# The last norm of an experts stage moved from VectorE to ScalarE, a tile per unit, its statistics spread over three units

## The chip, the cores and the metric

One core of a Trainium2 chip runs the whole program. The metric is device microseconds of one execution, as the median of several runs. The engines are named in the profile as PE (TensorE matmul), PEld (its weight loads), DVE (VectorE), ACT (ScalarE), POOL (GpSimd) and SP (SyncE, which here issues all DMAs). Each engine works through its own queue in order, and waits on semaphores that other engines raise.

## The reference

The program is a decoder of six sub-layers over 8192 tokens of width 128, each followed by a residual add and a layer norm without gain. The change touches the last, a mixture of experts with a shared expert:

```python
x = _layernorm(x + _L1_ffn_ref(x, ...), axis=-1)      # the output

def _layernorm(x, axis=-1, eps=1e-05):
    m = jnp.mean(x, axis=axis, keepdims=True)
    v = jnp.var(x, axis=axis, keepdims=True)
    return (x - m) / jnp.sqrt(v + eps)

# _L1_ffn_ref: 64 experts of inner width 64, a router's weight coef per token and expert
g = jnp.einsum('th,ehi->tei', x, Wg)
u = jnp.einsum('th,ehi->tei', x, Wu)
h = jax.nn.silu(g) * u * coef[:, :, None]
moe_out = jnp.einsum('tei,eih->th', h, Wd)
shared = jax.nn.silu(x @ SWg) * (x @ SWu) @ SWd       # inner width 128
return (moe_out + shared).reshape(orig_shape)
```

## The kernel before

The experts are computed in `phase_moe`, the last stage of the program. Tokens are taken 512 at a time (a group; 16 groups, `steps` = 8 turns of `U` = 2). The 64 experts go in 32 pairs of 2 x 64 inner columns, and the shared expert is the 33rd, so a group has `UNITS` = 33 units. Within a unit, everything is transposed: features or inner columns on the 128 partitions, 512 tokens along the free axis. Values are split into a high and a low f16 part, and each product is three f16 matmuls (`thrice`).

The steps of unit u, by engine:

- PE, `up`: 6 matmuls from `x_high` and `x_low` into two PSUM tiles `ps_g` and `ps_u`, of which there are two each. It therefore waits until the unit two before has been read out of them, by ScalarE (`silu_ready`) and by VectorE (`upper_ready`).
- ACT, `gate`: silu of `ps_g` into `gated`.
- DVE, `weigh`: `ps_u` times the router's weights (`coef`, loaded by DMA 4 units at a time) into `upper`.
- POOL, `join`: `hidden` = `gated` x `upper`.
- ACT, `high_h`, and DVE, `low_h`: the two f16 parts of `hidden`. Both are issued two units later (`HALVED` = 2).
- PE, `down`: 3 matmuls into the group's PSUM tile `ps_o`, four units later (`LAG` = 4).

So the order in which the queues take their work is, in a unit: PE `up(u)`, `down(u-4)`; ACT `gate(u)`, `high_h(u-2)`; DVE `weigh(u)`, `low_h(u-2)`; POOL `join(u)`. `hidden`, `gated`, `upper` and the f16 parts have `NB` = 6 buffers.

What is left of the previous group is put between the units of the next one, by constants that hold the number of a unit. In unit `COPY_OUT` = 4 ScalarE copies `ps_o` to `oT`. In unit `TURN` = 5 TensorE transposes it back to tokens on partitions, four 128x128 tiles. In unit `ADD` = 6 VectorE adds the residual `x_sb` into `y`, and goes on with four `bn_stats`, four `bn_aggr` and `var_eps` = variance + epsilon. In unit `POWER` = 7 GpSimd raises it to -1/2 (`rstd`). In unit `NORM` = 9 VectorE makes the result, four instructions of one 128x128 tile each:

```python
dve.wait_ge(rstd_ready, nth(it, j))
dve.wait_ge(stored[s], 16 * (it + 1) if j >= 0 else 16 * it)
for q in range(QT):
    last = nc.vector.tensor_scalar(res[s][:, q, :], y[s][:, q, :], mv[s][:, q, 0:1], rstd[s][:, q:q + 1], ALU.subtract, ALU.mult)
```

SyncE stores `res` after it has issued the coefficient loads 0 to 6 of the group's 8 (`store`, on `y_ready`). In unit `PREP` = 16 ScalarE and GpSimd split the next group's `xT` into its parts. After the last group, `drain` does the rest of the work with nothing beside it.

Of the kernel before, what the change touches and what calls it, by code (L numbers as in the profile page):

```python
# [9 lines left out]
ACT = mybir.ActivationFunctionType  # L10
ALU = mybir.AluOpType
# [5 lines left out]
P = 128  # L17
# [2484 lines left out]
def phase_moe(nc, w, x5, x5T, coefT, out):  # L2502
# [6 lines left out]
    U, GROUP, LAG, HALVED = 2, 512, 4, 2  # L2509
    QT = GROUP // P  # L2510
# [1 line left out]
    NB = 6  # L2512
    CU, CBUFS = 4, 4
    CHUNKS = PAIRS_E // CU
    PREP, COPY_OUT, TURN, ADD, POWER, NORM = 16, 4, 5, 6, 7, 9

    with Phase(nc, "d2") as ph:
        def slots(name, shape, dt=F32):
            return [ph.sb(f"{name}{j}", shape, dt) for j in range(U)]
# [9 lines left out]
        oT, y, res = slots("oT", [D, GROUP]), slots("y", [P, QT, D]), slots("res", [P, QT, D])  # L2529
        bn, mv = slots("bn", [P, QT, 6]), slots("mv", [P, QT, 2])  # L2530
        var_eps, rstd = slots("var_eps", [P, QT]), slots("rstd", [P, QT])
        minus_half = ph.sb("minus_half", [P, QT])
        ps_g = [ph.ps(f"g{i}", [P, GROUP]) for i in range(2)]
        ps_u = [ph.ps(f"u{i}", [P, GROUP]) for i in range(2)]
# [3 lines left out]
        coef_loaded = [ph.sem(f"coef_loaded{i}") for i in range(CBUFS)]  # L2538
        stored = [ph.sem(f"stored{j}") for j in range(U)]
        names = ("consts", "x_high_ready", "x_low_ready", "gu_ready", "silu_ready", "upper_ready", "h_ready", "h_high_ready",  # L2540
                 "h_low_ready", "down_done", "oT_copied", "turned", "x_added", "var_ready", "rstd_ready", "y_ready", "dve_own", "waited")
        (consts, x_high_ready, x_low_ready, gu_ready, silu_ready, upper_ready, h_ready, h_high_ready,
         h_low_ready, down_done, oT_copied, turned, x_added, var_ready, rstd_ready, y_ready, dve_own, waited) = (
            ph.sem(n) for n in names)

        def nth(it, j):

            return U * it + j + 1
# [40 lines left out]
        with nc.Block() as block:  # L2589
# [40 lines left out]
            @block.gpsimd  # L2630
            def _(pool):
                nc.gpsimd.memset(minus_half[:], -0.5).then_inc(consts, 1)
                pool.wait_ge(consts, 1)

                def power(it, j):
                    s = j % U
                    pool.wait_ge(var_ready, nth(it, j))
                    nc.gpsimd.tensor_tensor(rstd[s][:], var_eps[s][:], minus_half[:], ALU.pow).then_inc(rstd_ready, 1)

                def low_x(it, j):  # L2640
                    pool.wait_ge(x_high_ready, nth(it, j))
                    if not is_first(it):
                        pool.wait_ge(gu_ready, unit(it, j, UNITS - 1) - UNITS * U)
                    nc.gpsimd.tensor_tensor(x_low[j][:], xT[j][:], x_high[j][:], ALU.subtract).then_inc(x_low_ready, 1)  # L2644

                def join(it, j, u):
                    b = pos(j, u) % NB
                    pool.wait_ge(silu_ready, unit(it, j, u))
                    pool.wait_ge(upper_ready, unit(it, j, u))
                    after(pool, h_low_ready, it, j, u, NB)  # L2650
                    nc.gpsimd.tensor_tensor(hidden[b][:], gated[b][:], upper[b][:], ALU.mult).then_inc(h_ready, 1)  # L2651

                def group(it, j, following, previous):
                    for u in range(UNITS):
                        join(it, j, u)
                        if u == PREP and following is not None:
                            low_x(*following)
                        if u == POWER and previous is not None:
                            power(*previous)
                looped(nc.gpsimd, lambda: low_x(0, 0), group, power)  # L2660
# [48 lines left out]
            @block.scalar  # L2709
            def _(act):  # L2710
                def high_x(it, j):
                    act.wait_ge(xT_loaded[j], 16 * (it + 1))
                    if not is_first(it):
                        act.wait_ge(gu_ready, unit(it, j, UNITS - 1) - UNITS * U)
                    nc.scalar.activation(x_high[j][:], xT[j][:], ACT.Copy).then_inc(x_high_ready, 1)

                def gate(it, j, u):
                    i, b = pos(j, u) % 2, pos(j, u) % NB
                    act.wait_ge(gu_ready, unit(it, j, u))
                    after(act, h_ready, it, j, u, NB)  # L2720
                    nc.scalar.activation(gated[b][:], ps_g[i][:], ACT.Silu, scale=1.0 / W_SCALE).then_inc(silu_ready, 1)  # L2721

                def high_h(it, j, u):
                    b = pos(j, u) % NB
                    act.wait_ge(h_ready, unit(it, j, u))
                    after(act, down_done, it, j, u, NB)
                    nc.scalar.activation(h_high[b][:], hidden[b][:], ACT.Copy).then_inc(h_high_ready, 1)  # L2727

                def copy_out(it, j):
                    s = j % U  # L2730
                    act.wait_ge(down_done, unit(it, j, UNITS - 1))
                    nc.scalar.activation(oT[s][:], ps_o[s][:], ACT.Copy, scale=1.0 / (W_SCALE * H_SCALE)).then_inc(oT_copied, 1)

                def group(it, j, following, previous):
                    for u in range(UNITS):
                        gate(it, j, u)
                        lagging = earlier(it, j, u, HALVED)
                        if lagging is not None:
                            high_h(*lagging)
                        if u == PREP and following is not None:  # L2740
                            high_x(*following)
                        if u == COPY_OUT and previous is not None:
                            copy_out(*previous)

                def drain(it, j):
                    for u in range(UNITS - HALVED, UNITS):
                        high_h(it, j, u)
                    copy_out(it, j)
                looped(nc.scalar, lambda: high_x(0, 0), group, drain)

            @block.vector
            def _(dve):
# [16 lines left out]
                def add(it, j):  # L2769
                    s, number = j % U, nth(it, j)  # L2770
                    dve.wait_ge(turned, number)
                    dve.wait_ge(x_loaded[s], 16 * (it + 1) if j >= 0 else 16 * it)
                    nc.vector.tensor_tensor(y[s][:], ps_o[s][:].rearrange("p (q d) -> p q d", q=QT), x_sb[s][:], ALU.add).then_inc(x_added, 1)
                    dve.wait_ge(x_added, number)
                    for q in range(QT):
                        last = nc.vector.bn_stats(bn[s][:, q, :], y[s][:, q, :])
                    last.then_inc(dve_own, 1)
                    dve.wait_ge(dve_own, 2 * number - 1)
                    dve.sem_inc(waited, 1)
                    for q in range(QT):  # L2780
                        last = nc.vector.bn_aggr(mv[s][:, q, :], bn[s][:, q, :])
                    last.then_inc(dve_own, 1)
                    dve.wait_ge(dve_own, 2 * number)
                    nc.vector.tensor_scalar(var_eps[s][:], mv[s][:, :, 1], EPS_OUT, None, ALU.add).then_inc(var_ready, 1)

                def norm(it, j):
                    s = j % U
                    dve.wait_ge(rstd_ready, nth(it, j))

                    dve.wait_ge(stored[s], 16 * (it + 1) if j >= 0 else 16 * it)  # L2790
                    for q in range(QT):
                        last = nc.vector.tensor_scalar(res[s][:, q, :], y[s][:, q, :], mv[s][:, q, 0:1], rstd[s][:, q:q + 1], ALU.subtract, ALU.mult)  # L2792
                    last.then_inc(y_ready, 1)

                def group(it, j, following, previous):
                    for u in range(UNITS):
                        weigh(it, j, u)
                        lagging = earlier(it, j, u, HALVED)
                        if lagging is not None:
                            low_h(*lagging)  # L2800
                        if u == ADD and previous is not None:
                            add(*previous)
                        if u == NORM and previous is not None:
                            norm(*previous)

                def drain(it, j):
                    for u in range(UNITS - HALVED, UNITS):
                        low_h(it, j, u)
                    add(it, j)
                    norm(it, j)  # L2810
                for j in range(U):
                    dve.sem_inc(stored[j], 16)
                looped(nc.vector, lambda: None, group, drain)
# [105 lines left out]
```

## Time and profile before

| | us |
|---|---|
| median of 3 runs | 4137.38 |
| lowest and highest | 4135.95, 4141.83 |
| the profiled execution, its own time | 4147.94 |
| its span in the trace | 4146.2 |
| TensorE busy in the span | 3539.4 |
| VectorE busy | 3134.3 |
| ScalarE busy | 2357.5 |
| GpSimd busy | 1846.6 |

The experts' stage is roughly the last 1090 us of the span, from 3058.85 us, where its first matmul starts. A line number of the profile is that of `before.py`. In a timeline each row has the start, the duration, the engine, line and operation, out<-in by the program's names (`d_` for this stage's tiles, buffer numbers left out), and in brackets the idle time ahead of it and what ended it. A row with a count above one (x4) merges neighbours: its duration is from the start of the first to the end of the last. Matmuls are pipelined, and their recorded durations overlap.

### The profile page before, as it was taken

The numbers are of one execution on the slowest core, as the hardware profiler recorded it, in microseconds if no ns is written. First come the engines' busy times: TensorE is split into PE (matmuls) and PEld (weight loads), VectorE is DVE, ScalarE is ACT, GpSimd is POOL, SyncE is SP. The second block draws the span as 40 slices with busy tenths as digits, with TensorE's granted clock in tenths as the row PEclk, the third lists the DMA queues.
The fourth block names the chain that finished last, engine by engine and source line by source line (L and its number), as shares of the span: only waits on it lengthen the run. The fifth ranks groups of instructions, "written<-read, shape, count | busy, mean of one in ns | idle before, by whom it ended". The sixth has DMA issues, their size and how long they took to land. (4 is left out here: it accounts for less than half of the span.)

```text
span 4146.2 us, 92196 instructions
## 1 busy us (share of the span) xinstructions
PE 3539.4 (85%) x30917; PEld 2304.7 (56%) x30917; DVE 3134.3 (76%) x6483; ACT 2357.5 (57%) x5257; POOL 1846.6 (45%) x2322
## 2 busy tenths in 40 slices
PE   6899999997675863988999886888759999999998
PEld 3466666664445762666666665777624444444443
DVE  6677777775764654888888885888868888888887
ACT  1455555555672443777777774656545555555555
POOL 1000000002553653556565652222237878787876
PEclk9999999998886875677777777888879999999999
DMA  2000000001112211000000002222165666666664
GB/s 79 7 10 10 10 10 10 10 9 32 46 44 76 66 35 33 16 15 14 15 13 15 15 8 54 57 56 55 46 166 136 139 135 140 133 143 133 136 137 87
DMA packets 279448, 243.73 MB, mean 59 GB/s; under 512 B 57832, under 2 KB 205324, under 8 KB 279308
## 3 DMA queue, kind: packets, MB, share of 16 engines
q1 hardware_dynamic: 267916, 237.21, 24.1%
q10 hardware_dynamic: 11392, 4.79, 0.5%
q8 instruction: 70, 1.15, 0.1%
q14 instruction: 70, 0.57, 0.1%
HBM read 210.34 MB, written 31.59 MB: 58 GB/s over the span
## 5 line engine op out<-in xcount | busy, mean ns | idle before, releaser
L2651 POOL TENSOR_TENSOR d_hidden<-d_gated,d_upper 128x512 f32<-128x512 f32 x528 | 802.7, 1545 | 228.5 <-DVE d_upper L2760 103.5
L2767 DVE TENSOR_TENSOR d_h_low<-d_hidden,d_h_high 128x512 f16<-128x512 f32 x528 | 540.7, 1024 | 119.1 <-ACT d_h_high L2727 117.9
L2721 ACT ACTIVATE d_gated<-d_g 128x512 f32<-128x512 f32 x528 | 315.4, 597 | 461.4 <-PE d_u L2667 461.4
L750 POOL MEMSET f_minus_half<- 128x4 f32 x1 | 0.1, 103 | 866.5 <-POOLq L37 866.5
L2760 DVE TENSOR_TENSOR d_upper<-d_u,d_coef 128x512 f32<-128x512 f32 x512 | 349.3, 682 | 29.0 <-DMA d_coef<-coefT 10.3
L2727 ACT ACTIVATE d_h_high<-d_hidden 128x512 f16<-128x512 f32 x528 | 328.4, 622 | 8.1 <-POOL d_hidden L2651 8.1
L1824 ACT ACTIVATE c_sc<-c_sc,c_negmax 128x129 f32<-128x129 f32 x1024 | 326.2, 393 | 11.7 <-issue 7.7
L1652 POOL TENSOR_TENSOR c_posg<-w_pos,c_gate 128x512 f32<-128x512 f32 x256 | 266.3, 1041 | 0.0
L2665 PE MATMUL d_g<-d_x_high,w_Wg_high 128*128 128x512 f16 x528 | 200.5, 380 | 73.2 <-POOL d_x_low L2644 37.3
L1829 ACT ACTIVATE c_pT<-c_turned 128x512 f32<-128x512 f32 x256 | 149.8, 585 | 156.1 <-PE c_turned L1731 155.9
L1731 PE MATMUL c_turned<-all_ident,c_sc 128*128 128x128 f32 x1024 | 227.2, 361 | 8.2 <-ACT c_sc L1824 7.4
L2665 PE MATMUL d_o<-d_h_high,w_Wd_high 128*128 128x512 f16 x528 | 200.1, 379 | 2.0 <-ACT d_h_high L2727 1.6
L2666 PE MATMUL d_u<-d_x_high,w_Wu_low 128*128 128x512 f16 x528 | 200.4, 379 | 0.0
L2667 PE MATMUL d_u<-d_x_low,w_Wu_high 128*128 128x512 f16 x528 | 200.4, 379 | 0.0
L2665 PE MATMUL d_u<-d_x_high,w_Wu_high 128*128 128x512 f16 x528 | 200.3, 379 | 0.0
L2667 PE MATMUL d_g<-d_x_low,w_Wg_high 128*128 128x512 f16 x528 | 200.3, 379 | 0.0
L2666 PE MATMUL d_g<-d_x_high,w_Wg_low 128*128 128x512 f16 x528 | 200.3, 379 | 0.0
L2667 PE MATMUL d_o<-d_h_low,w_Wd_high 128*128 128x512 f16 x528 | 200.1, 379 | 0.0
L2666 PE MATMUL d_o<-d_h_high,w_Wd_low 128*128 128x512 f16 x528 | 200.1, 379 | 0.0
L1731 PEld LDWEIGHTS c_turned<-all_ident,c_sc 128*128 128x128 f32 x1024 | 147.5, 181 | 65.6 <-issue 49.1
L1936 DVE TENSOR_REDUCE c_top<-c_sc 128x4 f32<-128x516 f32 x256 | 177.0, 691 | 8.8
L1723 PE MATMUL c_scores<-c_rows 24*128 24x128 f16 x1024 | 160.8, 290 | 17.8 <-DVE c_sc L1934 17.7
(409 smaller groups left out, 9900.6 us busy)
## 6 DMA issues: line engine op xcount, KB each, us to landing
d_coef<-coefT SPq DMA_DIRECT2D x256, 512.0 KB, 7.3
d_cT<-in_ctxT SPq DMA_DIRECT2D x128, 64.0 KB, 2.0
mx_x<-in_xT SPq DMA_DIRECT2D x16, 256.0 KB
b_x<-in_x SPq DMA_DIRECT2D x64, 64.0 KB
y<-b_y SPq DMA_DIRECT2D x64, 64.0 KB, 1.6
f_y<-y SPq DMA_DIRECT2D x16, 256.0 KB, 3.3
f_x<-in_x SPq DMA_DIRECT2D x16, 256.0 KB, 3.8
x<-f_res SPq DMA_DIRECT2D x16, 256.0 KB, 2.4
```

The source lines that it names most:

```text
L1652: nc.gpsimd.tensor_tensor(posg[a][:], w["pos"][:, hs, :], gate[s][:, hs].unsqueeze(2).to_broadcast([T, 4, T]), ALU.mult).then_inc(posg_rea ...
L1731: last = nc.tensor.transpose(tbank[a % 2][:, i, :], sc[slot(j)][:, 4 * a + i, 0:T], w["ident"][:])
L1824: last = nc.scalar.activation(sc[s][:, h, :], sc[s][:, h, :], ACT.Exp, bias=negmax[s][:, h:h + 1], scale=SCALE)
L1936: m = own.mark(nc.vector.tensor_reduce(top[s][:, hs], sc[s][:, hs, :], AX, ALU.max))
L2651: nc.gpsimd.tensor_tensor(hidden[b][:], gated[b][:], upper[b][:], ALU.mult).then_inc(h_ready, 1)
L2665: nc.tensor.matmul(out, weights[0], high, start=start, stop=False)
L2666: nc.tensor.matmul(out, weights[1], high, start=False, stop=False)
L2667: return nc.tensor.matmul(out, weights[0], low, start=False, stop=stop)
L2721: nc.scalar.activation(gated[b][:], ps_g[i][:], ACT.Silu, scale=1.0 / W_SCALE).then_inc(silu_ready, 1)
L2727: nc.scalar.activation(h_high[b][:], hidden[b][:], ACT.Copy).then_inc(h_high_ready, 1)
L2760: nc.vector.tensor_tensor(upper[b][:], ps_u[i][:], coef[c % CBUFS][:, u % CU, :], ALU.mult).then_inc(upper_ready, 1)
L2767: nc.vector.tensor_tensor(h_low[b][:], hidden[b][:], h_high[b][:], ALU.subtract).then_inc(h_low_ready, 1)
```

## The change

- The last norm goes from VectorE to ScalarE. It is done as `Identity(y * rstd + offset)` with offset = -mean * rstd, one 128x128 tile in each of the units `NORM` to `NORM` + 3, which are now 12 to 15. The first of them waits for `offset_ready`, the last raises `y_ready`.
- VectorE makes `minus_mean` (128x4, one more instruction), GpSimd multiplies it by `rstd` into `offset` (128x4, one more instruction, behind a wait for its own `rstd`).
- VectorE's work in unit 6 is cut up: the add stays in unit 6, two `bn_stats` go to unit 7, two to unit 8, and `bn_aggr`, `minus_mean` and `var_eps` to unit 9.
- GpSimd's power goes from behind `join(7)` to behind `join(10)`. `PREP` goes from 16 to 17.
- VectorE's wait for the store of the group two before (`stored`) goes from the norm to the add.

```diff
-    PREP, COPY_OUT, TURN, ADD, POWER, NORM = 16, 4, 5, 6, 7, 9
+    PREP, COPY_OUT, TURN, ADD, POWER, NORM = 17, 4, 5, 6, 10, 12
...
+        minus_mean, offset = slots("minus_mean", [P, QT]), slots("offset", [P, QT])
...
                     nc.gpsimd.tensor_tensor(rstd[s][:], var_eps[s][:], minus_half[:], ALU.pow).then_inc(rstd_ready, 1)
+                    pool.wait_ge(rstd_ready, nth(it, j))
+                    nc.gpsimd.tensor_tensor(offset[s][:], minus_mean[s][:], rstd[s][:], ALU.mult).then_inc(offset_ready, 1)
...
+                def norm(it, j, q):
+                    s = j % U
+                    if q == 0:
+                        act.wait_ge(offset_ready, nth(it, j))
+                    last = nc.scalar.activation(res[s][:, q, :], y[s][:, q, :], ACT.Identity, bias=offset[s][:, q:q + 1], scale=rstd[s][:, q:q + 1])
+                    if q == QT - 1:
+                        last.then_inc(y_ready, 1)
...
                         if u == COPY_OUT and previous is not None:
                             copy_out(*previous)
+                        if NORM <= u < NORM + QT and previous is not None:
+                            norm(*previous, u - NORM)
...
                     copy_out(it, j)
+                    for q in range(QT):
+                        norm(it, j, q)
...
                     dve.wait_ge(x_loaded[s], 16 * (it + 1) if j >= 0 else 16 * it)
+                    dve.wait_ge(stored[s], 16 * (it + 1) if j >= 0 else 16 * it)
                     nc.vector.tensor_tensor(y[s][:], ps_o[s][:].rearrange("p (q d) -> p q d", q=QT), x_sb[s][:], ALU.add).then_inc(x_added, 1)
-                    dve.wait_ge(x_added, number)
-                    for q in range(QT):
+
+                def stats(it, j, qs):
+                    s = j % U
+                    if qs[0] == 0:
+                        dve.wait_ge(x_added, nth(it, j))
+                    for q in qs:
                         last = nc.vector.bn_stats(bn[s][:, q, :], y[s][:, q, :])
-                    last.then_inc(dve_own, 1)
+                    if qs[-1] == QT - 1:
+                        last.then_inc(dve_own, 1)
+
+                def gather(it, j):
+                    s, number = j % U, nth(it, j)
                     dve.wait_ge(dve_own, 2 * number - 1)
                     dve.sem_inc(waited, 1)
                     for q in range(QT):
                         last = nc.vector.bn_aggr(mv[s][:, q, :], bn[s][:, q, :])
                     last.then_inc(dve_own, 1)
                     dve.wait_ge(dve_own, 2 * number)
+                    nc.vector.tensor_scalar(minus_mean[s][:], mv[s][:, :, 0], -1.0, None, ALU.mult)
                     nc.vector.tensor_scalar(var_eps[s][:], mv[s][:, :, 1], EPS_OUT, None, ALU.add).then_inc(var_ready, 1)
-
-                def norm(it, j):
-                    s = j % U
-                    dve.wait_ge(rstd_ready, nth(it, j))
-
-                    dve.wait_ge(stored[s], 16 * (it + 1) if j >= 0 else 16 * it)
-                    for q in range(QT):
-                        last = nc.vector.tensor_scalar(res[s][:, q, :], y[s][:, q, :], mv[s][:, q, 0:1], rstd[s][:, q:q + 1], ALU.subtract, ALU.mult)
-                    last.then_inc(y_ready, 1)
...
-                        if u == NORM and previous is not None:
-                            norm(*previous)
+                        if u == ADD + 1 and previous is not None:
+                            stats(*previous, (0, 1))
+                        if u == ADD + 2 and previous is not None:
+                            stats(*previous, (2, 3))
+                        if u == ADD + 3 and previous is not None:
+                            gather(*previous)
```

## Rows read from the trace of the kernel before

**Rows 1.** The page: busy time of TensorE, and its granted clock in 40 slices.
```profile
PE 3539.4 (85%) x30917; PEld 2304.7 (56%) x30917; DVE 3134.3 (76%) x6483; ACT 2357.5 (57%) x5257; POOL 1846.6 (45%) x2322
...
PEclk9999999998886875677777777888879999999999
```

**Rows 2.** Busy time by window, one period of the stage.
```profile
3277.20:3344.40 67.20, 64.86 (x301) 29.38 (x301) 58.77 (x82) 37.95 (x68) 52.93 (x35) 1.00 0.67 137
```

**Rows 3.** Waits of TensorE, 3050 to 4146 us: total us, times, longest.
```profile
PE d_g L2665 <- DVE d_upper L2760: 35.9, 31, 1.5
...
PE d_o L2665 <- DVE d_h_low L2767: 0.4, 1, 0.4
```

**Rows 4.** Timeline of TensorE: four of its 31 waits; start, duration, [idle before].
```profile
3064.47 0.38 PE L2665 MATMUL d_g<-d_x_high,w_Wg_high 128*128 128x512 f16 x1 [1.40 <-DVE d_upper L2760]
...
3277.47 0.38 PE L2665 MATMUL d_g<-d_x_high,w_Wg_high 128*128 128x512 f16 x1 [1.25 <-DVE d_upper L2760]
...
3284.50 0.38 PE L2665 MATMUL d_g<-d_x_high,w_Wg_high 128*128 128x512 f16 x1 [1.04 <-DVE d_upper L2760]
...
4090.48 0.38 PE L2665 MATMUL d_g<-d_x_high,w_Wg_high 128*128 128x512 f16 x1 [1.04 <-DVE d_upper L2760]
```

**Rows 5.** Timeline of VectorE, 3271 to 3285 us.
```profile
3274.28 0.68 DVE L2773 TENSOR_TENSOR d_y<-d_o,d_x 128x512 f32<-128x512 f32 x1
3274.99 0.87 DVE L2776 BATCH_NORM_STATS2 d_bn<-d_y 128x6 f32<-128x128 f32 x4
3276.02 0.38 DVE L2781 BATCH_NORM_AGGREGATE d_mv<-d_bn 128x2 f32<-128x6 f32 x4 [0.16 <-DVE d_bn L2776]
3276.43 0.17 DVE L2784 TENSOR_SCALAR d_var_eps<-d_mv 128x4 f32<-128x4 f32 x1
3276.63 0.69 DVE L2760 TENSOR_TENSOR d_upper<-d_u,d_coef 128x512 f32<-128x512 f32 x1
...
3280.72 3.03 DVE L2792 TENSOR_SCALAR d_res<-d_y,d_mv,d_rstd 128x128 f32<-128x128 f32 x4
3283.67 0.68 DVE L2760 TENSOR_TENSOR d_upper<-d_u,d_coef 128x512 f32<-128x512 f32 x1
```

**Rows 6.** Timeline of ScalarE, 3271 to 3285 us.
```profile
3273.66 0.60 ACT L2721 ACTIVATE d_gated<-d_g 128x512 f32<-128x512 f32 x1 [0.83 <-PE d_u L2667]
3274.16 0.62 ACT L2727 ACTIVATE d_h_high<-d_hidden 128x512 f16<-128x512 f32 x1
3275.61 0.60 ACT L2721 ACTIVATE d_gated<-d_g 128x512 f32<-128x512 f32 x1 [0.83 <-PE d_u L2667]
```

**Rows 7.** Timeline of GpSimd, 3271 to 3285 us.
```profile
3270.93 2.88 POOL L2651 TENSOR_TENSOR d_hidden<-d_gated,d_upper 128x512 f32<-128x512 f32 x2 [1.28 <-ACT d_gated L2721]
...
3279.01 1.46 POOL L2638 TENSOR_TENSOR d_rstd<-d_var_eps,d_minus_half 128x4 f32<-128x4 f32 x1
```

**Rows 8.** Tile views: count, then duration in ns: least/median/greatest, of three operations.
```profile
L2792 DVE TENSOR_SCALAR d_res<-d_y,d_mv,d_rstd x64: 332/339/1310, 3146.4 to 4141.7; 128x128 f32<-128x128 f32 x64
...
L2767 DVE TENSOR_TENSOR d_h_low<-d_hidden,d_h_high x528: 673/749/1805, 3067.1 to 4134.5; 128x512 f16<-128x512 f32 x176
...
L2651 POOL TENSOR_TENSOR d_hidden<-d_gated,d_upper x528: 1254/1598/1812, 3064.5 to 4132.0; 128x512 f32<-128x512 f32 x176
```

**Rows 9.** Timeline of all engines at the end, 4137 to 4146 us.
```profile
4140.97 1.11 DVE L2792 TENSOR_SCALAR d_res<-d_y,d_mv,d_rstd 128x128 f32<-128x128 f32 x4 [1.12 <-POOL d_rstd L2638]
```

**Rows 10.** Timelines of GpSimd and ScalarE near 1505 us, an earlier stage's norm.
```profile
1505.37 1.04 POOL L1057 TENSOR_TENSOR b_rstd<-b_rstd,b_minus_half 128x4 f32<-128x4 f32 x1
1506.48 0.20 POOL L1059 TENSOR_TENSOR b_offset<-b_offset,b_rstd 128x4 f32<-128x4 f32 x1
...
1506.72 1.65 ACT L1210 ACTIVATE b_x<-b_y,b_offset,b_rstd 128x128 f32<-128x128 f32 x4 [0.80 <-POOL b_offset L1059]
```

**Rows 11.** Groups of ScalarE instructions, whole kernel: table loads (busy us, mean ns).
```profile
L236 ACT ACT_TABLE_LOAD x1 | 1.3, 1283 | 2.0 <-PEq L141 2.0
...
L2721 ACT ACT_TABLE_LOAD x1 | 1.3, 1283 | 0.0
```

More of the change, by code:

```diff
@@ L2540, in phase_moe @@
         names = ("consts", "x_high_ready", "x_low_ready", "gu_ready", "silu_ready", "upper_ready", "h_ready", "h_high_ready",
-                 "h_low_ready", "down_done", "oT_copied", "turned", "x_added", "var_ready", "rstd_ready", "y_ready", "dve_own", "waited")
+                 "h_low_ready", "down_done", "oT_copied", "turned", "x_added", "var_ready", "rstd_ready", "offset_ready", "y_ready", "dve_own", "waited")
         (consts, x_high_ready, x_low_ready, gu_ready, silu_ready, upper_ready, h_ready, h_high_ready,
-         h_low_ready, down_done, oT_copied, turned, x_added, var_ready, rstd_ready, y_ready, dve_own, waited) = (
+         h_low_ready, down_done, oT_copied, turned, x_added, var_ready, rstd_ready, offset_ready, y_ready, dve_own, waited) = (
             ph.sem(n) for n in names)
@@ L2809, in drain @@
                     add(it, j)
-                    norm(it, j)
+                    stats(it, j, range(QT))
+                    gather(it, j)
                 for j in range(U):
```

## The prediction

> **What bounds the kernel now.** I read the page first, for the busy shares, then the last stage in windows, then the waits of TensorE, then its timeline beside those of the other engines. TensorE is busiest, and over the stage's slices (from the 30th) its granted clock is near full, against tenths of 5 to 8 in the slices before [rows 1]; one period of the stage shows 1.00, that is 2.4 GHz, so the clock gives and costs nothing here. That period is 67.20 us wide and TensorE is busy for 64.86 of it, VectorE 58.77, ScalarE 37.95, GpSimd 52.93 [rows 2]. So TensorE bounds the stage, and what it could give is its idle time of 2.3 us in each group.
>
> The waits say where this is. TensorE's `d_g` matmul waits 35.9 us in 31 times, always for `d_upper`, VectorE's multiplication [rows 3]. The timeline has one such wait at the stage's start (1.40 us), and then 15 pairs, one in each later group, the last one ending at 4090.48: near 3277 us a wait of 1.25 and one of 1.04 [rows 4]. I take their sum as 35.9 - 1.40 = 34.5 us, 2.30 a group, which is the idle time of rows 2.
>
> VectorE's timeline names both causes [rows 5]. The first: in unit 6 it does the add, four `bn_stats`, four `bn_aggr` and `var_eps` in a row from 3274.28 to 3276.60, and `upper(7)` starts only at 3276.63. TensorE takes it up at 3277.47, 0.15 after its end at 3277.32. Without the wait TensorE would have gone at 3277.47 - 1.25 = 3276.22, so the latest harmless start of `upper(7)` is 3276.22 - 0.15 - 0.69 = 3275.38. The second: in unit 9 the four norm tiles hold VectorE from 3280.72 for 3.03 us. A norm tile takes 339 ns in the median, but 1310 at most [rows 8]; alone at the end the four take 1.11 us [rows 9].
>
> **The change part by part.** Units are 1.945 us apart when nothing stalls (two gates, 3273.66 and 3275.61 [rows 6]), so the latest harmless starts of `upper` are 3275.38, 3277.32, 3279.27 and 3281.21 for units 7 to 10, and 3288.99 for unit 14. I lay the new work on this grid, with the durations of rows 5 to 8; where VectorE's `low_h` can meet a GpSimd operation I take 0.69 as the one end and 1.72 as the other (least 673 ns, median 749, greatest 1805 [rows 8]).
>
> *Statistics.* Unit 6 ends with the add at 3274.95. `upper(7)` starts there, 0.43 early. `low_h(5)` follows at 3275.6 with GpSimd idle (`hidden(7)` needs `upper(7)`), ends at 3276.2; two `bn_stats` take 0.87/2 = 0.45; `upper(8)` starts at 3276.7, 0.6 early. `low_h(6)` may lie behind `hidden(7)` until 3278.0; two more `bn_stats`; `upper(9)` at 3278.5, 0.8 early. `low_h(7)` ends by 3279.8 behind `hidden(8)`. `bn_aggr` and `var_eps` took 0.74 from the end of the stats (3275.86 to 3276.60), and `minus_mean` is one more 128x4 instruction, at most the 0.17 of `var_eps`: 0.9, so `upper(10)` starts at about 3280.7, 0.5 early. The first wait, 1.25, goes: 15 x 1.25 = 18.8 us. The instructions are as many as before; their cover is VectorE's own idle time, 67.20 - 58.77 = 8.4 us a group, now met in several units.
>
> *The norm off VectorE.* 3.03 us a group leave it, and 0.17 come. The second wait, 1.04, goes: 15.6 us. Both together are bounded by the 34.5 of above, the term that I use.
>
> *The norm on ScalarE.* No row of this stage has it; the same shape and operation in an earlier stage takes 1.65 us for four, so one adds 0.39 to a row of them and 0.49 alone [rows 10]. A unit of ScalarE is 0.60 and 0.62, and it idles 0.83 ahead of each gate [rows 6]. 0.49 fits in 0.83: nothing on the path. If the cover were gone, 0.39 x 4 = 1.6 us a group.
>
> *GpSimd.* The power is the same instruction, 1.46 beside VectorE's work [rows 7], 1.04 alone [rows 10]. The offset costs 0.20 and 0.07 of waiting [rows 10]; I bound it by 0.27 and 0.45. GpSimd idles 67.20 - 52.93 = 14.3 us a group, which hides it.
>
> *The handoffs behind `join(10)`, where it is tightest.* `upper(10)` ends at 3281.4, `hidden(10)` by 3282.8 to 3283.2, the power by 3284.2 to 3284.7, the offset by 3284.5 to 3285.2. The first norm tile stands in ScalarE's unit 12, behind `high_h(10)` and ahead of `gate(13)`, which is due at 3285.33 and may start 1.8 late (3276.07 - 0.60 for unit 7, against its gate at 3273.66). The tile ends by 3285.7: no stall. `hidden(11)` waits behind power and offset and ends at 3286.1 to 3286.9; `high_h(11)` 0.7 later; `low_h(11)`, ahead of `upper(14)` in VectorE's queue, starts at 3286.8 to 3287.6 and ends 0.69 to 1.72 later, 3287.5 to 3289.3. The latest harmless start of `upper(14)` is 3288.99. So there are 1.5 us to spare at the one end and 0.3 missing at the other. I take 0 (nearest to it is the median `low_h` of 0.75, which leaves over half a microsecond) and keep 0.3 to 0.4 a group, 15 x 0.4 = 6 us, for the range.
>
> One of these numbers hangs on whether `minus_mean` can be held up as the norm tiles were. `var_eps`, its neighbour, takes 0.17 with GpSimd idle [rows 5, 7]. The Trainium skill (GPSIMD Engine Reference, Key points) says that GpSimd shares its SBUF interfaces with VectorE and contends with instructions that read two SBUF inputs or use a two-port mode. The spread of the norm tile and of `low_h` in rows 8 agrees; whether a 128x4 instruction is held, no row shows. Held to the end of `hidden(9)`, about 3281.0, it would put `upper(10)` 0.2 ahead of its limit instead of 0.5, and the sum stays.
>
> *SyncE.* `y_ready` comes with the last tile, in unit 15, at about 3291, some 7 us later than now. The store stands ahead of the load of coefficient chunk 7, which has to wait for `upper(15)` (issued near 3289.9) anyway and is used only in unit 28, 25 us later: nothing. The wait for `stored`, now in the add, is for a store issued a whole group before. `PREP` one unit later leaves 15 units until its result is used.
>
> *The end.* In `drain` nothing is hidden. `minus_mean` adds 0.08 (the step of a `bn_aggr`: (0.38 - 0.15)/3) to 0.17; the offset 0.27; the four tiles 1.65 on ScalarE instead of 1.11 [rows 9, 10]: together +0.9 us.
>
> **Sum.** -34.5 + 0.9 = -33.6 us. The profiled execution's own 4147.94 would become 4114.3 (span 4146.2 to 4112.6). The median of the runs is 10.56 below the profiled one; less 33.6 it is 4103.8, so **4104 us**, -0.81%. A change of 0.2%, 8 us, is about what a measurement of this kernel can tell from none.
>
> **Rivals.**
>
> *Part of the stall stays.* Three margins (0.43 at `upper(7)`, 0.5 at `upper(10)`, 0.3 missing at worst at `upper(14)`) are thinner than one `hidden` (1.6), and a delay in one unit pushes the next. For it: VectorE is busy 58.77 of 67.20, and `low_h` swings by a microsecond. Against: in the other 31 units TensorE never waits. With 1.0 us a group left, 4104 + 15 = 4119.
>
> *The wait moves to `down`.* Power and offset together put `hidden(11)` 1.7 to 1.9 us back, and `down(11)` needs `low_h(11)` by about 3289. If that is late by all that was gained, 2.2 us a group, the time is 4104 + 33 = 4137. For it: the worst end above. Against: it would need `low_h(11)` at 3291, two GpSimd operations later than my worst, and that wait is 0.4 us in the whole stage now [rows 3].
>
> *The other side: ScalarE reloads its table.* Silu and Identity now alternate in units 12 to 15. If they don't share a table, each of the four tiles costs two loads of 1.283 us [rows 11], and a unit of ScalarE grows by 2.57 + 0.39 against the 0.83 that it idles: 2.1 late a unit, 8.5 in four, less the 1.8 that a gate may be late, 6.7 a group, 15 x 6.7 = 100 us: 4204 us. One load in four tiles would already take back most of the gain; it decides from a lateness of 1.8 + 2.3 us. Against it: the stage has a single load although Silu and Copy alternate in it, and the rest of the kernel has one in all, with Identity in it [rows 10, 11]. The Trainium skill (ScalarE: Activation LUTs, Table sets: the hidden batching unit) says that cheap functions, identity and copy among them, lie in every set, and prices a load at about 2.7 us; the trace has 1.283 for a load, and that Identity is in Silu's set no row shows.
>
> **How the numbers follow.** Chances: both waits gone, 0.8 (4101 to 4110: the runs before spread over 6 us, and 6 for a leftover at unit 14); part stays, 0.11; moved to `down`, 0.05; table loads or another wait on ScalarE of more than 4 us, 0.04. The predicted time is the first's. The range, 4100 to 4119, takes in the second case up to a microsecond a group. Faster by over 0.2%: 0.8 + 0.11 = 0.91; within: 0.05; slower: 0.04.
>
> **What the profile after would show.** TensorE's wait for `d_upper` 1 to 2 us in one or two times in place of 35.9 in 31; a period of 64.9 us; no wait for `d_h_low` or `d_h_high` beyond today's; `d_res` on ScalarE at 0.49 us; `d_offset` on GpSimd at 0.20 to 0.36 us; `upper(7)` to `upper(10)` less than 1.1 us after they are due; ScalarE with one table load in the stage; the last store 0.9 us later after the last matmul. Wrong would make it: a wait of `d_g` or `d_o` left in each group, near units 9, 12 or 16; a period over 66 us; `hidden(11)` ending later than 1.8 us behind its place.

## The result, and the profile after

The changed kernel takes 4100.15 us in the median of 6 runs (4095.53 to 4102.84), the one before 4138.38 in 6 (4135.95 to 4141.83): 38.2 us less. The ratio is 0.9905, 95% interval 0.9892 to 0.9918. The direction and the mechanism are as forecast, the size is not: 33.6 us were forecast. The range, 4100 to 4119 us, was worked out from a median before of 4137.38 us; as a gain it is 18.4 to 37.4 us, and the measured 38.2 lies just beyond it.

The page of the changed kernel, busy times and TensorE's granted clock in 40 slices:

```profile
PE 3529.7 (86%) x30917; PEld 2302.4 (56%) x30917; DVE 3103.1 (76%) x6435; ACT 2378.3 (58%) x5321; POOL 1857.0 (45%) x2338
...
PEclk9999999998887775767776777888869999999999
```

Of VectorE's work 31 us are gone, ScalarE has 21 more [rows 1]. The span, 4094.1 us, is 52.1 shorter than that of before, more than the medians differ, so the two profiled executions can't be compared as a whole. The stage can be: from its first matmul to the end of its last store it takes 1045.2 us (3045.47 to 4090.67) where it took 1083.65 (3058.85 to 4142.50), 38.45 less. Of the other 13.6 us of the spans' difference, 13.4 come ahead of the stage, where the change touches nothing, and 0.3 behind its last store.

The waits of TensorE from 3040 us on (engine, tile and line, who ended the wait: us in total, times, longest):

```profile
...
PE d_o L2668 <- ACT d_h_high L2730: 1.6, 2, 0.9
PE d_g L2668 <- DVE d_upper L2775: 1.2, 1, 1.2
...
PE d_o L2668 <- DVE d_h_low L2782: 0.4, 1, 0.4
```

Both waits for `d_upper` are gone from all 15 groups; the one that stays is the one at the stage's start [rows 3, 4]. A window as wide as one period of the changed kernel has nothing but matmuls on TensorE (columns as in [rows 2]):

```profile
3300.00:3364.54 64.54, 64.54 (x303) 29.50 (x302) 56.55 (x78) 39.32 (x73) 53.82 (x37) 1.00 0.62 143
```

The timeline of VectorE, units 6 to 10 of one group (upper(7), (8), (9) and (10) are the four rows of L2775 after the add):

```profile
3255.71 0.68 DVE L2791 TENSOR_TENSOR d_y<-d_o,d_x 128x512 f32<-128x512 f32 x1
3256.31 0.68 DVE L2775 TENSOR_TENSOR d_upper<-d_u,d_coef 128x512 f32<-128x512 f32 x1
3256.90 0.68 DVE L2782 TENSOR_TENSOR d_h_low<-d_hidden,d_h_high 128x512 f16<-128x512 f32 x1
3257.50 0.47 DVE L2798 BATCH_NORM_STATS2 d_bn<-d_y 128x6 f32<-128x128 f32 x2
3257.90 0.67 DVE L2775 TENSOR_TENSOR d_upper<-d_u,d_coef 128x512 f32<-128x512 f32 x1
...
3259.58 0.67 DVE L2775 TENSOR_TENSOR d_upper<-d_u,d_coef 128x512 f32<-128x512 f32 x1
...
3261.27 0.84 DVE L2810 TENSOR_SCALAR d_minus_mean<-d_mv 128x4 f32<-128x4 f32 x1
3262.02 0.16 DVE L2811 TENSOR_SCALAR d_var_eps<-d_mv 128x4 f32<-128x4 f32 x1
3262.09 0.68 DVE L2775 TENSOR_TENSOR d_upper<-d_u,d_coef 128x512 f32<-128x512 f32 x1
```

In place of one block of 2.3 us [rows 5] there are four small ones. `minus_mean` is held: 0.84 us for 128x4 elements, its median over the 16 groups is 830 ns and its least 169. The handoff behind it, on GpSimd and then on ScalarE:

```profile
3262.90 1.60 POOL L2654 TENSOR_TENSOR d_hidden<-d_gated,d_upper 128x512 f32<-128x512 f32 x1 [0.82 <-DVE d_upper L2775]
3264.46 1.46 POOL L2639 TENSOR_TENSOR d_rstd<-d_var_eps,d_minus_half 128x4 f32<-128x4 f32 x1
3266.00 0.70 POOL L2641 TENSOR_TENSOR d_offset<-d_minus_mean,d_rstd 128x4 f32<-128x4 f32 x1
3266.66 5.85 POOL L2654 TENSOR_TENSOR d_hidden<-d_gated,d_upper 128x512 f32<-128x512 f32 x4
```
```profile
3266.73 0.49 ACT L2741 ACTIVATE d_res<-d_y,d_offset,d_rstd 128x128 f32<-128x128 f32 x1 [0.82 <-POOL d_offset L2641]
3267.13 0.58 ACT L2724 ACTIVATE d_gated<-d_g 128x512 f32<-128x512 f32 x1
3267.95 0.63 ACT L2730 ACTIVATE d_h_high<-d_hidden 128x512 f16<-128x512 f32 x1 [0.24 <-POOL d_hidden L2654]
3268.49 0.48 ACT L2741 ACTIVATE d_res<-d_y,d_offset,d_rstd 128x128 f32<-128x128 f32 x1
```

ScalarE's gate(13) comes at 3267.13 in place of about 3266.75, and nothing on TensorE moves.

**Where the missing 5 us are.** Two neighbouring matmuls of before, and the row of four transposes that marks the same place in each group, in two neighbouring groups before and in two after:

```profile
3275.62 0.38 PE L2666 MATMUL d_o<-d_h_high,w_Wd_low 128*128 128x512 f16 x1
3275.84 0.38 PE L2667 MATMUL d_o<-d_h_low,w_Wd_high 128*128 128x512 f16 x1
...
3269.79 0.60 PE L2690 MATMUL d_o<-all_ident,d_oT 128*128 128x128 f32 x4
...
3336.94 0.60 PE L2690 MATMUL d_o<-all_ident,d_oT 128*128 128x128 f32 x4
```
```profile
3251.21 0.60 PE L2693 MATMUL d_o<-all_ident,d_oT 128*128 128x128 f32 x4
...
3315.75 0.60 PE L2693 MATMUL d_o<-all_ident,d_oT 128*128 128x128 f32 x4
```

Matmuls start 0.216 us apart but are recorded 0.38 long: neighbours overlap by 0.16. An idle time is counted from the recorded end of the matmul in front. The stalled matmul of [rows 4] starts at 3277.47, 1.63 after the one at 3275.84; without the wait it would have been 0.216. The wait cost 1.41 us, and its row says 1.25. So a period went from 67.15 to 64.54 us, by 2.61, where the two rows add up to 2.29. That each wait costs 0.16 us more than its row says is theory A of the experiments below; theory B is that it costs what the row says.

### The profile page after: what moved, and what is told of

It reads as the page before. It is cut to its first block and busy times, and to the rows that moved or that the text cites. A ratio compares the mean times of both kernels' runs of the same rounds, so it can differ in the third digit from the quotient of the medians.

```text
span 4094.1 us, 92236 instructions
## 1 busy us (share of the span) xinstructions
PE 3529.7 (86%) x30917; PEld 2302.4 (56%) x30917; DVE 3103.1 (76%) x6435; ACT 2378.3 (58%) x5321; POOL 1857.0 (45%) x2338
## 5 line engine op out<-in xcount | busy, mean ns | idle before, releaser
L2654 POOL TENSOR_TENSOR d_hidden<-d_gated,d_upper 128x512 f32<-128x512 f32 x528 | 812.5, 1565 | 174.4 <-DVE d_upper L2775 88.2
L2775 DVE TENSOR_TENSOR d_upper<-d_u,d_coef 128x512 f32<-128x512 f32 x512 | 348.5, 681 | 24.3 <-DMA d_coef<-coefT 10.2
```

The source lines that it names most:

```text
L2775: nc.vector.tensor_tensor(upper[b][:], ps_u[i][:], coef[c % CBUFS][:, u % CU, :], ALU.mult).then_inc(upper_ready, 1)
```

## The experiments

All start from the changed kernel. "Period" is the distance of the transposes of neighbouring groups, as above; it repeats within some hundredths in nearly all groups of a trace (in the Exp kernel it doesn't), so it tells apart what times of a whole run can't. The wait rows are those for `d_upper`, with the one at the stage's start among them; in "norm on ScalarE at once" and "power three times" they are those for `d_h_low`, in the Exp kernel those for `d_gated`. For timed kernels the ratio is to the kernel before on the same chip, with its 95% interval.

| kernel | period us | wait rows, us (times) | median us | ratio |
|---|---|---|---|---|
| before | 67.15 | 35.9 (31) | 4138.38 | 1 |
| changed | 64.54 | 1.2 (1) | 4100.15 | 0.9905 (0.9892-0.9918) |
| statistics at once | 65.96 | 19.8 (16) | 4125.09 | 0.9963 (0.995-0.9975) |
| norm on VectorE at once | 65.75 | 17.0 (16) | 4117.97 | 0.9949 (0.9933-0.9966) |
| norm on VectorE, a tile a unit | 66.38 | 18.5 (61) | 4127.75 | 0.9969 (0.9955-0.9983) |
| norm on VectorE, two units | 65.98 | 17.6 (31) | 4123.02, one run | |
| norm on ScalarE at once | 65.28 | 8.4 (18) | 4112.80 | 0.9935 (0.9919-0.9952) |
| power twice | 64.54 | 1.5 (2) | 4104.21 | 0.9904 (0.9882-0.9926) |
| power three times | 65.42 | 9.8 (16) | 4114.55 | 0.994 (0.9923-0.9956) |
| norm on ScalarE with Exp | 72.6 to 78.2 | 76.8 (65) | 4248.02, one run | |

**Each half alone: statistics at once.**

```diff
                         if u == ADD and previous is not None:
                             add(*previous)
-                        if u == ADD + 1 and previous is not None:
-                            stats(*previous, (0, 1))
-                        if u == ADD + 2 and previous is not None:
-                            stats(*previous, (2, 3))
-                        if u == ADD + 3 and previous is not None:
-                            gather(*previous)
+                            stats(*previous, range(QT))
+                            gather(*previous)
```

> The changed kernel with the statistics back in one block in unit 6 (the norm stays on ScalarE). Both theories expect one wait of TensorE for d_upper in each of 15 groups, near unit 9, and none near unit 12. Theory A, the forecast's error was in reading the wait's idle time as its price: matmuls start 0.216 us apart but are recorded 0.38 long, so a wait costs 0.16 more than its row says. The wait's row then says 1.25 to 1.45 (minus_mean adds 0.08 to 0.17 to the block), the period is 64.54 + 1.42 to 1.6, that is 65.96 to 66.15 us, and the time is 21 to 24 us above the changed kernel. Theory B, a wait costs what its row says and the stage's other 5 us came from elsewhere: the period is 65.8 to 66.0 and exceeds 64.54 by the row's own number.

One such wait a group came back, near unit 9; the waits, and the timeline's row for one of them:

```profile
PE d_g L2668 <- DVE d_upper L2775: 19.8, 16, 1.3
```
```profile
3270.74 0.38 PE L2668 MATMUL d_g<-d_x_high,w_Wg_high 128*128 128x512 f16 x1 [1.26 <-DVE d_upper L2775]
```

The row says 1.26, the period grew by 65.96 - 64.54 = 1.42: 0.16 more, theory A to the hundredth. Theory B has fallen: by the row's own number the period would be 65.80.

**The other half: the norm back on VectorE, four tiles in unit 12.** (In this and the two like it, `offset` and `minus_mean` are left out, since nothing reads them.)

```diff
+                def norm(it, j, qs):
+                    s = j % U
+                    if qs[0] == 0:
+                        dve.wait_ge(rstd_ready, nth(it, j))
+                    for q in qs:
+                        last = nc.vector.tensor_scalar(res[s][:, q, :], y[s][:, q, :], mv[s][:, q, 0:1], rstd[s][:, q:q + 1], ALU.subtract, ALU.mult)
...
+                        if u == NORM and previous is not None:
+                            norm(*previous, range(QT))
```

> The changed kernel with the norm back on VectorE, all four tiles in unit 12, statistics spread as changed. The norm holds VectorE for about 3 us, so a wait for d_upper near unit 15 comes back in each group: a row of 1.0 to 1.8 us. Theory A: period longer than 64.54 by that row plus 0.16, time 18 to 30 us above the changed kernel. Theory B: period longer by the row alone. If the two parts of the change are independent, this and the kernel with the statistics at once together lose about the 39 us that the change gained.

```profile
PE d_g L2666 <- DVE d_upper L2761: 17.0, 16, 1.2
```

One wait a group and the one at the start: (17.0 - 1.2)/15 = 1.05 each; the period grew by 1.21, again 0.16 more. The halves are worth 1.42 and 1.21 us a group, together 2.63 against the 2.61 of the whole: they add up, so neither needs the other.

The wait came as expected, though not for the 3 us that I had put on the norm: in this trace the four tiles take 2.05 us (3273.82 to 3275.87), as one of them is held and not two, but the `low_h` ahead of them is held too and takes 1.67. So it is what a unit of VectorE holds in all that counts, not the length of the norm alone.

**The same, a tile a unit on VectorE,** in units 12 to 15: `if NORM <= u < NORM + QT` and `norm(*previous, (u - NORM,))`.

> The norm on VectorE, but a tile a unit in units 12 to 15, statistics spread. Theory S, what mattered is that no unit of VectorE is longer than TensorE's slack: a tile adds 0.26 to 1.2 us to a unit, against margins of 0.6 to 1.5 us in the changed kernel's trace, so at most 0.5 us a group comes back; period 64.54 to 65.0, time 0 to 7 us above the changed kernel. Rival, the engine matters, because VectorE's tile meets GpSimd and ScalarE's doesn't: 1 us a group or more, 15 us or more above the changed kernel.

My theory fell and the rival holds: 66.38, 1.84 a group over the changed kernel, and worse than four tiles at once. VectorE's timeline in two of these units, and GpSimd's:

```profile
3281.37 0.68 DVE L2761 TENSOR_TENSOR d_upper<-d_u,d_coef 128x512 f32<-128x512 f32 x1
3281.97 0.68 DVE L2768 TENSOR_TENSOR d_h_low<-d_hidden,d_h_high 128x512 f16<-128x512 f32 x1
3282.57 1.28 DVE L2803 TENSOR_SCALAR d_res<-d_y,d_mv,d_rstd 128x128 f32<-128x128 f32 x1
3283.77 0.68 DVE L2761 TENSOR_TENSOR d_upper<-d_u,d_coef 128x512 f32<-128x512 f32 x1
```
```profile
3282.18 1.59 POOL L2652 TENSOR_TENSOR d_hidden<-d_gated,d_upper 128x512 f32<-128x512 f32 x1 [0.82 <-ACT d_gated L2722]
3284.59 1.59 POOL L2652 TENSOR_TENSOR d_hidden<-d_gated,d_upper 128x512 f32<-128x512 f32 x1 [0.82 <-DVE d_upper L2761]
```

The tile starts while `hidden` runs and ends at 3283.85, 0.08 after it. Every unit has a `hidden`, and all 60 tiles that had a unit of their own were held (only the four behind the last group weren't): the tile view gives 1287 ns in the median where four at once have 336. So a unit becomes 3283.77 - 3281.37 = 2.40 us long against TensorE's 1.945, four times over: 4 x 0.46 = 1.84. TensorE's rows give the same with theory A: 18.5 us in 61 waits, (18.5 - 1.2)/60 = 0.29 each, and 4 x (0.29 + 0.16) = 1.80.

**Two tiles in each of two units,** `(0, 1)` in unit 12 and `(2, 3)` in unit 13.

> The norm on VectorE, two tiles in each of units 12 and 13, statistics spread. With all four in one unit the period was 65.75 us and only the first tile was held by GpSimd (1.28, then 0.34 each); with a tile a unit it was 66.38 and each of the four was held (1.28). Theory H, each unit with a norm tile pays one hold of about 1 us: here two holds, so two tiles of 1.28 and two of 0.34, and a period between the two, 65.8 to 66.2. Rival, it is only how long VectorE's longest unit is: the period falls below 65.75.

```profile
3275.43 2.52 DVE L2803 TENSOR_SCALAR d_res<-d_y,d_mv,d_rstd 128x128 f32<-128x128 f32 x2
...
3279.07 1.54 DVE L2803 TENSOR_SCALAR d_res<-d_y,d_mv,d_rstd 128x128 f32<-128x128 f32 x2
```

The period, 65.98, is between the two, where theory H had it. But the pairs show three holds in 14 of the 15 groups, not two: in the first pair both tiles were held, by two `hidden` in a row. So its number was met with a wrong count: how many holds there are depends on where GpSimd stands, not on the number of units alone. None of the three ways on VectorE that were tried comes near ScalarE's 64.54.

**The norm on ScalarE at once:** `if u == NORM`, `for q in range(QT): norm(*previous, q)`.

> The norm on ScalarE, all four tiles in unit 12. They end 1.2 us later than one tile does, gate(13) starts 0.1 us before its limit, and high_h(11), low_h(11) come about 1.0 us later, against a margin of 0.57 us before down(11) in the changed kernel's trace. Theory S: TensorE waits 0.3 to 0.6 us for d_h_low near unit 15, period 64.9 to 65.1, 5 to 9 us above the changed kernel. Rival, ScalarE's idle time hides it whole: period 64.54 and no difference.

```profile
PE d_o L2668 <- DVE d_h_low L2783: 8.4, 18, 0.5
PE d_g L2668 <- DVE d_upper L2776: 1.0, 1, 1.0
```

The wait came where it was expected, about 0.5 us for `d_h_low` in each group, and the period grew by 0.74, above my 0.3 to 0.6: I had once more taken the row for the price, 0.49 + 0.16 = 0.65. The other 0.1 is a wait of `up(12)`, as `upper(10)` came that much too late in this trace. It has no wait row at all, since it is shorter than the overlap; the distance of the two starts, 0.32 in place of 0.216, shows it:

```profile
3339.38 0.38 PE L2670 MATMUL d_o<-d_h_low,w_Wd_high 128*128 128x512 f16 x1
3339.70 0.38 PE L2668 MATMUL d_g<-d_x_high,w_Wg_high 128*128 128x512 f16 x1
```

A tile a unit is worth 0.74 us a group on ScalarE, where it was worth less than nothing on VectorE.

**How tight the handoff behind unit 10 is: the power twice.**

```diff
+                    nc.gpsimd.tensor_tensor(offset[s][:], var_eps[s][:], minus_half[:], ALU.pow)
                     nc.gpsimd.tensor_tensor(rstd[s][:], var_eps[s][:], minus_half[:], ALU.pow).then_inc(rstd_ready, 1)
```

> The changed kernel with the power of 128x4 done a second time on GpSimd ahead of the real one (its result is overwritten). GpSimd idles over 11 us a group. If that hides it (the forecast's rule for GpSimd), the period stays 64.54. If the handoff behind unit 10 is the tight place, as the changed kernel's trace has it (low_h(11) ends 0.57 us before down(11) needs it), 1.0 to 1.46 us more there give TensorE a wait of 0.5 to 0.9 us for d_h_low in each group: period 65.0 to 65.5, 7 to 13 us above the changed kernel.

```profile
3277.85 1.45 POOL L2639 TENSOR_TENSOR d_offset<-d_var_eps,d_minus_half 128x4 f32<-128x4 f32 x1
3279.27 1.00 POOL L2640 TENSOR_TENSOR d_rstd<-d_var_eps,d_minus_half 128x4 f32<-128x4 f32 x1
3280.35 0.20 POOL L2642 TENSOR_TENSOR d_offset<-d_minus_mean,d_rstd 128x4 f32<-128x4 f32 x1
```

No new wait in the groups, period 64.54. That is the number of the branch in which GpSimd's idle time hides the power, and the wait that I expected by the other is missed; but this run doesn't tell the two apart, since less was added than I had put in. With the second power GpSimd's three small operations take from 3277.85 to 3280.55, 2.70 us, against 2.24 (3264.46 to 3266.70) before: 0.46 more, not 1.0 to 1.46, because the second power takes only 1.00 and the offset drops from 0.70 to 0.20. `low_h(11)` came 0.48 later against its limit; 0.09 us of the margin were left.

**Three times,** the first into a tile that nothing reads.

> The changed kernel with the power of 128x4 done three times on GpSimd (the results of the first two are overwritten or unused). With it done twice the period stayed 64.54 us, but low_h(11) ended only 0.09 us before its limit, against 0.57 in the changed kernel. If that margin is what matters, a third power of 1.0 to 1.46 us goes past it: TensorE waits 0.6 to 1.3 us for d_h_low or d_upper near units 15 to 17 in each group, the period is 65.3 to 66.0, the time 11 to 22 us above the changed kernel. If GpSimd's idle time of some 11 us a group hides it as it hid the second one, the period stays 64.54.

```profile
PE d_o L2671 <- DVE d_h_low L2785: 9.8, 16, 0.6
```

Now it is past the margin: 65.42, 0.88 a group, by a wait for `d_h_low` in each group (0.63, and 0.16), the rest by `gate(13)` some 0.08 too late. So it is not GpSimd's idle time that hides this work but the margin of half a microsecond at one place.

**The price of the table rival:** `ACT.Exp` in place of `ACT.Identity` in the norm, so that the output is the exponential of the reference's.

> The changed kernel with Exp in place of Identity in the last norm, so that its output is the exponential of the reference's. It prices the rival of the forecast on the other side. If Exp is not in Silu's table: about 8 table loads of 1.28 us a group, and by the forecast's working 6.7 us a group, some 100 us in all. If one table serves both: no loads and the changed kernel's time.

```profile
L2724 ACT ACT_TABLE_LOAD x61 | 78.3, 1283 | 0.5
L2741 ACT ACT_TABLE_LOAD x61 | 78.3, 1283 | 1.1
```
```profile
3343.80 0.60 ACT L2724 ACTIVATE d_gated<-d_g 128x512 f32<-128x512 f32 x1 [6.01 <-issue]
```
```profile
3161.40:3165.00 3.60, 3.60 (x10) 1.22 (x9) 3.56 (x5) 2.64 (x6) 2.32 (x2) 0.53 0.75 200
...
3166.00:3190.00 24.00, 24.00 (x113) 10.88 (x111) 19.93 (x25) 14.01 (x26) 20.15 (x14) 1.00 0.57 132
```

Eight loads a group, and the stage takes 1190.0 us, 144.8 more than the changed kernel's 1045.2: 9.7 us a group, not 6.7. In the shortest groups the period is 72.6, 8.1 over the changed kernel's: that is the price of the four units with loads. The rest comes unevenly, from two things that the other kernels don't have. In five groups ScalarE also stands still for 3.9 to 6.0 us near the end (the row with [6.01]), for a reason that the profile doesn't show, and TensorE then waits up to 3.3 us for `d_gated`. And in 11 places TensorE's granted clock falls to half, 1.2 GHz, for 3.4 us; each time TensorE comes out of a wait for `d_gated` of 1.4 us or more (the first ends at 3160.94). The windows (columns as in [rows 2]) show one such stretch at a mean of 0.53 and the time behind it at 1.00. Matmuls then start 0.43 us apart in place of 0.216; a later wait of the group can hide this whole, and a group with such a stretch that is not hidden, and no standstill, is 1.0 us longer (73.6).

In the changed kernel the stage has one table load, so Identity and Silu share a table, as the Trainium skill has it (ScalarE: Activation LUTs, Table sets: the hidden batching unit). Its figure of about 2.7 us for a load is not what this trace has: 1.283 for each, and the next instruction starts 0.01 after it.

## Why the prediction came out as it did

1. *The price of the waits, the step that failed.* The prediction said of the waits "I take their sum as 35.9 - 1.40 = 34.5 us". The term is 15 x 2.61 = 39.2: each of the 30 waits cost 0.16 more than its row, 4.8 us in all. The period of 64.9 us that it forecast came out as 64.54. That the busy time of [rows 2] left the same 2.3 us was no second witness, since it rests on the same recorded durations. The period, 67.15 us from transposes to transposes, lay ready in the trace. It is the size of a term, not the mechanism; the kernels with the statistics at once and with the norm on VectorE at once show the 0.16 apart from the change itself, and the one with a tile a unit agrees. The same slip put the grid's limits too late: the stalled matmul would have started at 3277.47 - 1.41 = 3276.06 and not at 3276.22, so each margin forecast at VectorE's `upper` was 0.16 too wide.
2. *Both waits go.* Right: none is left in 15 groups, and each half alone brings back its own.
3. *Statistics.* Right in order and nearly in size. `upper(7)` ended 0.35 us before its limit (0.43 forecast), `upper(8)` 0.7 (0.6), `upper(9)` 0.96 (0.8), `upper(10)` 0.39 (0.5, or 0.2 with `minus_mean` held). Beside limits that are 0.16 earlier VectorE was even sooner than forecast.
4. *minus_mean.* Left open between 0.17 and a hold; it is held, 0.83. The Trainium skill (GPSIMD Engine Reference, Key points) names SBUF interfaces that the two engines share. The trace agrees in that the held instruction ends 0.03 us after GpSimd's `hidden` (3262.11 and 3262.08 us); whether it is of the kinds that the page lists no row shows.
5. *The norm on ScalarE.* 0.48 us a tile, hidden: right. The offset cost 0.70, above the 0.27 to 0.45 that I had bounded it by.
6. *The handoff behind unit 10.* The tightest place, as said, though at `down(11)`: 0.57 us to spare; `upper(14)` had 0.63. The reason given for GpSimd's part, that its idle time of 14.3 us a group hides it, was the wrong one: the third power was not hidden.
7. *The end.* Right: from the last transposes to the end of the last store 6.56 us (4084.11 to 4090.67), 5.68 before (4136.82 to 4142.50), 0.9 more.
8. *The rivals.* Neither a part of the stall nor a wait at `down` was left, and the table is loaded once in the stage.

The sum with the right price is -39.2 + 0.9, and -0.2 for the wait at the start (1.40 to 1.19): -38.5; the stage became 38.45 us shorter, the median of the runs 38.2.

Open is in part why Exp costs 9.7 us a group: a unit with two loads is 4.22 us long (3290.88, the first load, to 3295.10, the third), 2.28 over TensorE's, and four times that, less the 1.8 that a gate may be late, gives 7.3, where the shortest groups lose 8.1. What stops ScalarE in five groups is not shown; the worst of them loses 13.7 us. Which parts of a GpSimd operation hold VectorE was not taken apart either.

## What to carry to other kernels

Price a stall by the distance between starts, or by the period of the loop, not by the idle time of its row: where records overlap, the row is short by the overlap, here 0.16 us of 1.41, and a delay shorter than the overlap has no row. Side work in a pipelined loop is free only while each unit stays within the slack at its own place, so lay it on a grid of latest starts; the engine's idle share over the loop says little. Cutting work into a piece a unit helps on an engine that nothing holds, and can hurt on one where each piece meets a hold of its own; then put the pieces together, or on the other engine.

## What the runs showed of the hardware

- VectorE's 128x128 `tensor_scalar` from SBUF to SBUF takes 0.34 us alone and 1.28 when it meets GpSimd's multiplication. Even one of 128x4 goes from 0.17 to 0.83: `minus_mean` took 0.83 in all 15 groups of the changed kernel, where `hidden` runs beside it, and 0.17 in all of the kernel with the statistics at once, where GpSimd idles. That GpSimd is what holds it is read from such pairs.
- It works the other way too: GpSimd's power of 128x4 takes 1.00 us alone and 1.45 behind a `low_h`, and its 128x4 multiplication 0.20 to 0.70. Work added on GpSimd can therefore cost less than its own time: the second power added 0.46 us.
- `bn_stats`, `bn_aggr` and the operations with a PSUM operand were not held: 0.27 to 0.30, 0.14 to 0.18 and 0.67 to 0.69 us throughout the changed kernel's stage.
- 128x512 f16 matmuls at the full clock start 0.216 us apart and are recorded 0.38 long; at half the clock they start 0.43 us apart.
